# Cross-attention of a gated layer: other places for the token pieces, an earlier query copy, other banks

## The reference

```python
x = x + tanh(g_xattn) * xattn(layernorm(x), ctx)      # 16 heads of 128, q and k RMS-normed per head
y = layernorm(x)
# block on y: h = rmsnorm(y, ln1_w); causal self-attention, 16 heads of 128; y = y + ao @ wo
#             t = rmsnorm(y, ln2_w); 16 experts, 6 taken, 176 units each, and a shared one of 352
x = x + tanh(g_ffn) * block(y)
```

## Time and profile before

| | us |
|---|---|
| median of 3 runs | 637.55 (637.42 to 637.81) |
| the profiled execution, its own time | 637.76 |
| its span in the profile | 636.0 |
| TensorE busy | 623.6 |
| DVE busy | 463.0 |
| ACT busy | 320.5 |
| POOL busy | 252.8 |
| granted clock of TensorE | full in all slices |

### The profile page before, as it was taken

One profiled execution on the slowest core, in us unless ns is written; L12 is line 12 of the kernel. 1 busy time (PEld: TensorE's weight loads), 2 busy tenths in 40 slices (PEclk: granted clock), 3 DMA queues, 4 the chain that ended last, 5 costly groups with the idle time before them and its releaser, 6 DMA issues.

```text
span 636.0 us, 17180 instructions
## 1 busy us (share of the span) xinstructions
PE 623.6 (98%) x6688; PEld 544.8 (86%) x6688; DVE 463.0 (73%) x913; ACT 320.5 (50%) x699; POOL 252.8 (40%) x336
## 2 busy tenths in 40 slices
PE   8899999999999999999999999999999999999997
PEld 6688888877788998999999998988888888888886
DVE  5878877998886776876677788655556987555556
ACT  6777767677743335333344333354476444444443
POOL 3221121212132533444352444445554665555453
PEclk9999999999999999999999999999999999999999
DMA  7523131111011322222221331113323232333332
GB/s 225 189 64 89 51 97 33 33 46 37 17 51 34 116 73 81 69 67 68 68 87 48 108 91 39 35 51 99 88 87 98 78 101 84 92 97 99 94 90 90
DMA packets 36019, 50.24 MB, mean 79 GB/s; under 512 B 4080, under 2 KB 23024, under 8 KB 35952
## 3 DMA queue, kind: packets, MB, share of 16 engines
q1 hardware_dynamic: 35376, 48.81, 26.1%
q10 hardware_dynamic: 576, 0.48, 0.2%
HBM read 48.22 MB, written 1.05 MB: 77 GB/s over the span
## 4 chain that ended last, share of the span: by engine, by line
PE 88%; DVE 5%; ACT 3%; issue 1%; DMA 1%; SPq 0%; POOL 0%; DVEq 0%; ACTq 0%
PE acc L565 23%; PE bank_q L538 16%; PE bank_k L538 14%; PE bank_s L538 7%; PE bank_v L538 7%; PE bank_v L651 7%; PE bank_s L707 3%; PE bank_p L746 2%; PE bank_s L697 2%; PE bank_k L729 2%; PE bank_t L714 1%; PE bank_k L661 1%; PE bank_p L680 1%; PE bank_q L672 1%; DMA xt<-in_ctx_t 1%
## 5 line engine op out<-in xcount | busy, mean ns | idle before, releaser
L565 PE MATMUL acc<-wo_hi,pv_hi 128*128 128x256 f32 x328 | 93.4, 285 | 0.3 <-DVE pv_lo L1482 0.2
L565 PE MATMUL acc<-wo_lo,pv_hi 128*128 128x256 f32 x328 | 92.9, 283 | 0.0
L565 PE MATMUL acc<-wo_hi,pv_lo 128*128 128x256 f32 x328 | 92.1, 281 | 0.0
L1645 POOL TENSOR_TENSOR wq_lo<-raw_a,wq_hi 128x256 fp32r<-128x256 f32 x32 | 23.6, 738 | 121.2 <-DVE wq_hi L1419 121.2
L565 PEld LDWEIGHTS acc<-wo_hi,pv_hi 128*128 128x128 f32 x328 | 61.5, 188 | 4.9 <-issue 1.8
L1645 POOL TENSOR_TENSOR wq_lo<-raw_m,wq_hi 128x256 fp32r<-128x256 f32 x50 | 40.4, 808 | 60.5 <-DVE wq_hi L1438 59.0
L565 PEld LDWEIGHTS acc<-wo_lo,pv_hi 128*128 128x128 f32 x328 | 61.7, 188 | 2.3
L565 PEld LDWEIGHTS acc<-wo_hi,pv_lo 128*128 128x128 f32 x328 | 62.3, 190 | 0.0
L1482 DVE TENSOR_TENSOR pv_lo<-raw_a,pv_hi 128x512 fp32r<-128x512 f32 (+1 forms) x51 | 37.9, 745 | 33.3 <-ACT pv_hi L1086 33.0
L538 PE MATMUL bank_q<-xt_hi,wq_hi 128*128 128x512 f32 x144 | 59.9, 416 | 0.5 <-POOL wq_lo L1645 0.5
L1086 ACT ACTIVATE pv_hi<-raw_a 128x512 fp32r<-128x512 f32 (+1 forms) x51 | 31.7, 624 | 56.5 <-DVE raw_a L1477 50.8
(11 more groups left out here) (235 smaller groups left out, 1951.6 us busy)
## 6 DMA issues: line engine op xcount, KB each, us to landing
raw_m<-in_chunk_m SPq DMA_DIRECT2D x50, 256.0 KB, 2.7
raw_a<-in_head_a SPq DMA_DIRECT2D x48, 192.0 KB, 3.1
raw_b<-in_head_b SPq DMA_DIRECT2D x32, 256.0 KB, 3.3
raw_m<-in_chunk_m SPq DMA_DIRECT2D x50, 128.0 KB, 2.1
raw_v<-in_pair_v SPq DMA_DIRECT2D x16, 256.0 KB, 3.1
raw_b<-in_head_b SPq DMA_DIRECT2D x32, 128.0 KB, 2.1
xs<-in_x SPq DMA_DIRECT2D x6, 128.0 KB, 3.3
out<-xs SPq DMA_DIRECT2D x3, 256.0 KB, 2.4
```

The costliest lines, as they stand in the source:

```text
L565: last = nc.tensor.matmul(acc[t // 2][:, (t % 2) * D:(t % 2 + 1) * D], w[:, tok], m, start=begins and n == 0, stop=True, skip_group_check= ...
L1645: nc.gpsimd.tensor_tensor(lo, raw, hi, ALU.subtract).then_inc(signal, 1)
```

## The change

1. In `plan_of`, the token pieces of stage a on DVE move to slot 2, between subtraction and division: `norm` of x, half 1 (pair 5 of the first half); for y, half 0, the pieces `refine` and `centre` become one `norm` (pair 3 of the second half), `refine_root` and `apply` one `scale` (pair 5).
2. On DVE the copy `take_q(nxt, 0)` is ahead of slot 2 and the division; on ACT the square of those queries, `square_q(nxt, 0)`, is ahead of the second key copy.
3. The keys of the first two pairs use `bank_k` for head 0 and `bank_s` for head 1; keys 0 of the second pair don't wait for `raw`, keys 1 do. The first keys of self-attention use `bank_s` and `bank_q`, and wait for `raw` in place of `pv_lo`. The last pair's context products use another order of banks.
4. `norm_k` waits for `qt_1` in every pair but the first and writes to `bank_v` behind a pair with a `turn`. The wait for `xt_lo` moves from ahead of `norm_k` to ahead of the next pair's context products.
5. At the end of the last pair the first half of the values of self-attention is multiplied ahead of the context products, and ACT takes it ahead of the context values.
6. In a chunk `refine_root` and `apply` are done ahead of `split_hidden`.

```diff
--- before.py
+++ after.py
@@ -176,9 +176,9 @@
         for name, (i, slot) in places.items():
             pieces[kind, half, i, slot] = (name, step)
 
-    beside_pairs("a", 0, ("x", 1), stats=(pairs - 5, 2), norm=(pairs - 4, 1), turn=(pairs - 3, 0))
-    beside_pairs("a", 1, ("y", 0), stats=(1, 2), rough=(1, 1), refine=(2, 2), centre=(2, 1), sums=(3, 0), root=(3, 1),
-                 refine_root=(4, 2), apply=(4, 1), turn=(5, 0))
+    beside_pairs("a", 0, ("x", 1), stats=(pairs - 5, 2), norm=(pairs - 4, 2), turn=(pairs - 3, 0))
+    beside_pairs("a", 1, ("y", 0), stats=(1, 2), rough=(1, 1), norm=(2, 2), sums=(3, 0), root=(3, 1), scale=(4, 2),
+                 turn=(5, 0))
     beside_pairs("b", 0, ("y", 1), stats=(1, 1), norm=(2, 1), sums=(3, 0), root=(3, 1), scale=(4, 1), turn=(5, 0))
     beside_pairs("b", 1, ("t", 0), sums=(0, 1), root=(1, 0), scale=(1, 1), turn=(2, 0), logits=(3, 0), equals=(3, 1),
                  ties=(4, 0), better=(4, 1), ranks=(5, 0), best=(5, 1), weights=(6, 0), spread=(pairs - 1, 0))
@@ -395,14 +395,21 @@
 
         def context_bank(u, j):
 
-            return ((bank_k, bank_p, bank_t, bank_v) if u.deferred else (bank_v, bank_s, bank_p, bank_t))[j]
+            return (bank_k, bank_p, bank_t, bank_v if u.deferred else bank_s)[j]
 
         def context_of(u, j):
 
             return context_bank(u, j)[:, 0:HT // 2].rearrange("p (h n q) -> p h n q", h=2, q=SEQ)
 
         def key_bank(u, h):
-            return (bank_s, bank_k)[h] if u.kind == "a" else bank_k
+            if u.kind == "a":
+                return (bank_k, bank_s)[h] if u.n <= 2 else (bank_s, bank_k)[h]
+            return (bank_s, bank_q)[h] if u.very_first else bank_k
+
+        def key_sums(u):
+
+            turned = u.n > 1 and plan.piece(u.prev())[0] == "turn"
+            return (bank_v if turned else bank_p)[:, 0:HT // 2]
 
         def gate_bank(u):
             return (bank_q, bank_v)[u.parity]
@@ -625,8 +632,10 @@
 
                 stage, bank = stages[u.kind], key_bank(u, h)
                 pe.wait_ge(stage["wk_lo"], u.of(h))
-                if h and u.kind == "b":
+                if h and bank is bank_k and u.kind == "b":
                     pe.wait_ge(B["kt"], u.of(0))
+                if h and bank is bank_q:
+                    pe.wait_ge(B["qt"], u.of(1))
                 if u.kind == "a":
                     if u.needs_tokens and not h:
                         pe.wait_ge(ctxt_lo_ready, u.half + 1)
@@ -676,8 +685,10 @@
             def norm_k(u):
 
                 pe.wait_ge(A["sq_k"], u.of(1))
+                if not u.very_first:
+                    pe.wait_ge(A["qt_1"], u.n)
                 for j in range(QUADS):
-                    last = nc.tensor.matmul(bank_p[j * GROUP:(j + 1) * GROUP, 0:HT // 2], ones_of[:, 0:GROUP],
+                    last = nc.tensor.matmul(key_sums(u)[j * GROUP:(j + 1) * GROUP], ones_of[:, 0:GROUP],
                                             quads(sq_k[:])[:, :, :, j, :], start=True, stop=True)
                 last.then_inc(A["ssk_done"], 1)
 
@@ -786,6 +797,11 @@
                     return [(unit_w_ready, step[1] + 1)]
                 return []
 
+            def turned_tokens(u):
+
+                piece, step = piece_at(u)
+                return [(xt_lo_ready, KD * (PREP[step] + 1))] if piece == "turn" else []
+
             def release(held):
                 for semaphore, value in held:
                     pe.wait_ge(semaphore, value)
@@ -809,18 +825,22 @@
                     pe.wait_ge(A["ln_k"], u.n)
                     if prev.weighs_values:
                         pe.wait_ge(A["vo_lo"], prev.n)
+                    release(turned_tokens(prev))
                     context_values(prev)
                 if nxt.kind == "a":
-                    pe.wait_ge(A["raw"], u.n)
+                    if prev:
+                        pe.wait_ge(A["raw"], u.n)
                     project_keys(nxt, 0)
                 pe.wait_ge(A["ln_q"], u.n)
                 project_queries(nxt, 0)
-                if prev:
+                if nxt.kind == "b" or not prev:
+                    pe.wait_ge(A["raw"], u.n)
+                else:
                     pe.wait_ge(A["pv_lo"], QUADS * (prev.n - 1) + 1)
                 project_keys(nxt, int(nxt.kind == "a"))
                 if prev:
                     output(prev, 0)
-                held = prepare(u)
+                prepare(u)
                 if nxt.kind == "a":
                     project_queries(nxt, 1)
                 if prev:
@@ -828,17 +848,17 @@
                 if nxt.kind == "a":
                     if u.weighs_values:
                         value_out(u)
-                    release(held)
                     if not prev:
                         pe.wait_ge(A["ln_k"], u.n)
                     norm_k(nxt)
                 else:
                     project_queries(nxt, 1)
+                    project_values(nxt, False)
+                    pe.wait_ge(B["kt"], nxt.of(0))
                     context_values(u)
                     project_keys(nxt, 1)
-                    pe.wait_ge(A["pv_lo"], QUADS * (u.n - 1) + 2)
-                    project_values(nxt, False)
                     project_values(nxt, True)
+                    pe.wait_ge(A["pv_lo"], QUADS * u.n)
 
             def self_pair(u):
 
@@ -1029,7 +1049,7 @@
 
             def log_k(u):
                 act_e.wait_ge(A["ssk_done"], u.n)
-                nc.scalar.activation(half_wide[0], bank_p[:, 0:HT // 2], ACT.Ln, bias=eps5[:, 0:1]).then_inc(A["ln_k"], 1)
+                nc.scalar.activation(half_wide[0], key_sums(u), ACT.Ln, bias=eps5[:, 0:1]).then_inc(A["ln_k"], 1)
 
             def root_q(u):
 
@@ -1097,11 +1117,11 @@
                 take_k(nxt, 0)
                 if nxt.kind == "a":
                     square_k(nxt, 0)
+                    square_q(nxt, 0)
                     take_k(nxt, 1)
                 exponentials(u)
                 if nxt.kind == "a":
                     square_k(nxt, 1)
-                    square_q(nxt, 0)
                     if after.kind == "a":
                         round_keys(after, 0, nxt)
                 prepare(u)
@@ -1118,9 +1138,9 @@
                 if nxt.kind == "a":
                     log_k(nxt)
                 else:
+                    take_v(nxt, False)
                     take_context_values(u)
                     take_k(nxt, 1)
-                    take_v(nxt, False)
 
             def self_pair(u):
                 nxt = u.next()
@@ -1269,10 +1289,9 @@
                             last.then_inc(first_tokens, 1)
                     if PREP[step]:
                         last.then_inc(tok_ready, 1)
-                if piece in ("norm", "refine") and kind != "x":
+                if piece == "norm" and kind != "x":
                     await_root()
                     refined_root()
-                if piece in ("norm", "centre") and kind != "x":
                     for t in range(NT):
                         last = nc.vector.tensor_scalar(ys[:, half, t, :], xs[:, half, t, :], mv[:, t, 0:1],
                                                        st[:, 2, t:t + 1], ALU.subtract, ALU.mult)
@@ -1525,10 +1544,10 @@
                 if nxt.kind == "b":
                     split_values(nxt)
                     take_q(nxt, 0)
+                if nxt.kind == "a":
+                    take_q(nxt, 0)
                 prepare_piece(*piece_at(u, 2), u)
                 normalise(u)
-                if nxt.kind == "a":
-                    take_q(nxt, 0)
                 turn_weights(u)
                 split_queries(after, 0, nxt)
                 if after.kind == "b":
@@ -1543,7 +1562,6 @@
                     split_context_values(u)
                 if after.kind == "b":
                     split_keys(after, 1, nxt)
-                prepare_piece(*piece_at(u, 1), u)
                 if u.weighs_values:
                     split_value_out(u)
 
@@ -1600,7 +1618,7 @@
                 if nxt:
                     weigh_gate(nxt)
                     multiply_up(nxt)
-                with_scalar = piece_at(u)[0] in ("turn", "logits", "spread", "refine_root", "apply")
+                with_scalar = piece_at(u)[0] in ("turn", "logits", "spread")
                 if not with_scalar:
                     prepare_piece(*piece_at(u), u)
                 if nxt:
```

## The result

The changed kernel takes 631.46 us, the median of 4 runs (631.33 to 631.59), against 637.53 (637.42 to 637.81) for the kernel before on the same chip: ratio 0.9904, 95% interval 0.9887 to 0.9921, so 6.07 us faster. A second set of runs on another chip gave 631.65 against 637.79, the same ratio. The forecast was 632.6, a gain of 4.94.

A forecast was written before the change was run, and what follows sets the result against it. TensorE, busy 623.6 of 636.0 us, was taken as the bound, so only its idle stretches could change. Terms from 1.04 (first pair) to a loss of 0.35 summed to 4.94: 637.55 to 632.6, range 630.9 to 634.9.

The forecast's parts named there:

- the seven rows: TensorE's listed waits (sc_sub, qt, vs, one ahead of context products, wq_lo, xt_lo, pv_lo), about 6 us together.
- First pair: Cross-attention, first pair: keys no longer wait for bank_s and queries come earlier, less the new key-sum wait; gain 1.04.
- Second pair: Cross-attention, second pair's keys: DVE ready sooner, so the sc_sub wait shrinks; net gain 0.25, bounds 0 and 0.6.
- Centring of x: End of pair five, first half: centring moved behind the subtraction, so vo_lo no longer delays the context products; gain 0.62.
- Third and fourth pair of the second half: Normalisation of y no longer delays sc_sub, gain 0.65; new key-sum wait beside the squares of y, loss 0.35.
- The new wait in ordinary pairs: Second half, key sums waiting for the second query copy: fits by 0.15; five pairs cost 0 to 0.25, taken as 0.
- Fifth pair and turn of y: Second half: scaling of y no longer delays sc_sub, gain 0.78; key sums no longer wait for xt_lo, gain 0.5.
- Feed-forward: refine_root and apply ahead of the hidden split: gain 0.2, bounds −0.2 and 0.6; port rule 0.1, without it 0.6.
- Partly given back: Rival 1: ssq waits for GpSimd, key-sum wait costs 0.2 in five pairs; gain about 2.7, time 634.9, chance 0.16.
- No change: Rival 3: the first query square holds back ScalarE's second key copy; time within 0.2% (1.3 us), chance 0.05.
- Slower: Rival 4: the key sums' new wait binds in seven uncovered pairs; at 1.1 us late, 7.7 lost, time 640.3, chance 0.03.
- More than forecast: Rival 2: everything at its better bound and small bubbles of 0.1 vanish; gain 6.3 to 7, time 631, chance 0.08.

The follow-up runs named there:

- relieving that chain: Changed kernel, key-sum wait only behind a turn, second context split moved to third and fourth pair: 631.01 us; then first pair's vo_lo ahead of the casts too: 630.48 us.
- The slots alone: Kernel before with only the cross-attention token pieces moved behind the subtraction (five arguments of plan_of): 635.48 us, ratio 0.9963.
- the queries alone: Kernel before with only the earlier query copy on DVE and earlier query square on ScalarE: 635.55 us, ratio 0.9964.
- a short split: Changed kernel with GpSimd's rest of the down weights cut to 8 of 256 columns in two feed-forward chunks: 631.41 us in one run.

## Why the prediction was right, and where its sizes were off

*What bounds.* Right: the time came out of the seven rows and nothing downstream swallowed it. Every step that was forecast has its sign. What the profile after was to show came too: the waits that went, the two new ones of 0.84 and 0.79, one `sc_sub` of 0.21, the centring at 1.13, no wait in ordinary pairs. Only the sign for the feed-forward failed. No wait near 475 was to mean a gain of 0.6, but the product was late by a gap that the list doesn't show. The sum was 0.9 too low (5.86 against 4.94).

*First pair.* The size was right, 1.01 for 1.04, and one sentence of its reasoning holds only in part: "Gain: 1.04, out of 0.9 + 0.96 that stood there; the new wait takes the rest." At the second scores that is what happens, since without the wait the gain is 1.87. But the wait is not what the kernel pays for: without it the lead at the third scores is nearly the same (1.43 for 1.39), since `ln_k` and `sc_sub` of the second pair are then late. It was shown by taking the wait out, and by relieving that chain, after which 1.87 was kept.

*Second pair.* 0.38 for 0.25, inside its bounds; one `sc_sub` wait of 0.21 was left. `ssq` still took 0.75 beside GpSimd.

*Centring of x.* 0.73 for 0.62; the slots alone give 0.72 and the queries alone 0.39, so the time can't be put down to one of them. DVE's row after the change is one of 1.13 us in place of 2.51:

```profile
61.87 1.13 DVE L1287 TENSOR_SCALAR hn<-xs,mv 128x256 f32<-128x256 f32 x4
```

*Third and fourth pair of the second half.* The slots gave 0.67 for 0.65. The rotation of the attention weights came at 131.46 and the context products did not wait for it, DVE and TensorE after:

```profile
128.42 1.38 DVE L1296 TENSOR_SCALAR ys<-xs,mv,st 128x256 f32<-128x256 f32 x4
...
131.46 0.71 DVE L1420 STREAM_TRANSPOSE rows_t<-attn 128x512 f32<-128x512 f32 x1
```
```profile
133.88 0.27 PE L740 MATMUL bank_v<-rows_t,ctx_sb 32*128 32x128 f32 x1
134.08 0.50 PE L545 MATMUL bank_s<-ctxt_hi,wk_hi 128*128 128x512 f32 x1
```

The lead there is 2.79, so the rotation's end at 132.17 is 1.34 later against TensorE (133.62 less 2.79 is 130.83), where the forecast had 1.4. The keys follow the context products in 0.20, and the lead at the keys is 3.58: the whole 0.79 of the old wait is gained there. But 0.41 of it is lost again in the same pair, 0.19 at the second keys (a lead of 3.39) and 0.22 at the output product (3.17). Both wait for `pv_lo`, which starts at 135.87, behind a product of scores that takes 0.89 beside GpSimd's split and starts late. With the slots alone 0.22 is lost there. I had kept 0.15, at another place. At the key sums the lead then falls to 2.31. It comes back to 2.92 at the scores, since query sums and scores had waits of their own before, so the new wait costs 0.25 against the time before, where I had 0.35. So 0.79 - 0.41 - 0.25 is the 0.13 measured.

The term that failed here is the loss kept of the 0.79, 0.41 for 0.15. The new wait came out inside its bounds, but "Loss 0.35" is not what it costs in the changed kernel: without it the step is 0.97, so it takes 0.84 of what would be gained. The single parts don't add up to this: 0.67 (slots) + 0.44 (queries) - 0.86 (wait) is 0.25.

*The new wait in ordinary pairs.* Right at 0, but with less to spare than "It fits, by 0.15, of which a wait's own latency takes some 0.1" says. Where the wait binds, the sums start 0.15 behind the copy (142.49 to 142.64), so 0.15 is what the wait itself takes. In the first pair of the second half of the kernel with the wait alone the copy ends at 113.01 and the sums start at 113.17, 0.21 behind the last output product (112.96); in the kernel before they start 0.21 behind it too (112.91 to 113.12). The wait fits there with nothing in hand. Nor does the earlier query square bring any: in the changed kernel the copy ends at 110.50 and the sums start at 110.66. ScalarE's second square waits for TensorE's second queries in any case (its idle time before it was 0.51 and is now 0.99), so the copy keeps its distance to TensorE.

*Fifth pair and turn of y.* 1.56 for 1.28. The rows part it: 0.98 by the keys, where `sc_sub` was late, 0.06 by the output product and 0.50 at the key sums, where `xt_lo` was. The slots alone give 0.94; the 0.2 that I kept as a wait behind `ssq` did not come. The turn came at its size, but the earlier queries alone take 0.40 of that wait away, with the sums still waiting for `xt_lo`. How much the other bank was needed is open.

*Eleventh and twelfth scores.* Forecast 0, measured 0.33, and the queries alone give 0.33 from the tenth scores on. The term was missing. DVE and GpSimd of the kernel before, then of the kernel after, at the product of scores and query norms:

```profile
126.35 0.97 DVE L1370 TENSOR_TENSOR sc<-sc_sub,r_q 128x512 f32<-128x512 f32 x1
126.32 0.46 POOL L1645 TENSOR_TENSOR wk_lo<-raw_a,wk_hi 128x128 fp32r<-128x128 f32 x1
```
```profile
123.78 0.69 DVE L1389 TENSOR_TENSOR sc<-sc_sub,r_q 128x512 f32<-128x512 f32 x1
123.85 0.94 POOL L1663 TENSOR_TENSOR wk_lo<-raw_a,wk_hi 128x128 fp32r<-128x128 f32 x1
```

The split keeps its place: it starts 2.47 us earlier, which is the lead of the tenth scores. The product starts 2.57 earlier. That is 0.10 more, and puts it ahead of the split, so now the split is long (0.94 for 0.46) and the product isn't, and `pv_lo` behind it is no longer late. The kernel with the queries alone has the same pair of rows, 125.21 for 0.69 and 125.30 for 0.92. Before, the output product followed its predecessor in 0.33 and the next in 0.22; after, in 0.24 and 0.12. Such gaps are below what the list of waits shows, and that list was all I had priced. That GpSimd's hold is the cause here was argued from these rows, and not tried alone.

*Last pair.* 1.39 for 1.25, and 1.33 by that part alone.

*Feed-forward.* 0.39 for 0.2, between the port rule's 0.1 and the 0.6 without it. The old wait was worth about 0.7 from start to start (0.74 and 0.31 where 0.12 and 0.23 are dense) where I had 0.62, and the output product lost 0.32 where I had 0.5. The rows first: the root instruction that met the split took 0.58 and ended 0.01 behind it, the one that had started 0.01 before it took 0.16, and a short split removed the hold. The Trainium skill, "SBUF — State Buffer", section "SBUF: two separate sides", has the port locked for a whole instruction by whoever takes it first. The trace agrees. My reading of it was too coarse: "If the small instructions must wait for it" made all five follow the split, while here the first had run when it began, and only the second was held.

*Rivals.* Partly given back: no wait came in ordinary pairs and the third and fifth pair kept nothing. No change: ScalarE's second key copy did not hold the gain back, the queries alone gave 2.2 us. Slower: the wait alone costs 1.0 us, and for good in one pair of fifteen. It counts seven pairs with neither cover nor a place in the sum; they are six, since the first pair is in the sum too. More than forecast was the nearest, by 0.46; its "small bubbles of 0.1 that vanish with earlier DVE" are what was seen at the eleventh and twelfth scores.

## What to carry to other kernels

Where one engine bounds the kernel, count its gaps from start to start at a fixed mark of each stage, and keep the lead as a ledger: it separates parts of 0.1 us that single spans mix with the chance of the first load. The list of waits is not the whole ledger: gaps of 0.1 to 0.24 stood in none of its rows here. A wait removed pays only if the next stage's chain on the other engines is early as well, so look one stage further for what has its date from elsewhere. Where DVE and GpSimd meet, what a piece costs depends on where it is put (2.51 us or 1.13 for the same four instructions), so look at what GpSimd does in the stretch into which a piece is moved.

## Not expected of the hardware

A small DVE instruction that started at 465.94, 0.01 us before GpSimd's split, took its usual 0.16 us, and the next, which started inside the split, took 0.58. Which of the two is held may hang on so small a distance, but the two differ in form as well: the first reads one tensor, the second two, and no run here has the first start inside this split. So the order of the starts is not shown to decide here.

It goes the other way too. In the changed kernel GpSimd's split that starts at 468.33, while DVE multiplies `r_k` (468.16 to 468.85), took 1.12 us, where the same split takes 0.73 to 0.75 beside no such product:

```profile
468.33 1.12 POOL L1663 TENSOR_TENSOR wq_lo<-raw_m,wq_hi 128x256 fp32r<-128x256 f32 x1 [1.63 <-DVE wq_hi L1457]
```
